# GpSimd's row writes in twos, an earlier one-hot and an earlier bias in a two-stage attention and expert kernel

## The reference, cut to what matters

```
def reference(x, ctx, g_xattn, g_ffn, Wq, Wk, Wv, Wo, Wg, bg, W1, b1, W2, b2):
    x = x + tanh(g_xattn) * xattn(layernorm(x), ctx, Wq, Wk, Wv, Wo)
    x = x + tanh(g_ffn)   * ffn(layernorm(x), Wg, bg, W1, b1, W2, b2)
    return x

# xattn: 16 heads of 16. For each token the scores are between the 16 dims of Q and the
# 16 dims of K (a 16 x 16 softmax for each token), then values, then @ Wo.T
# ffn: 8 experts, each token goes to one:
    logits = xf @ Wg + bg ; idx = argmax(softmax(logits))
    h = gelu(xf @ W1[idx] + b1[idx]) ; out = h @ W2[idx] + b2[idx]
```

## Time and profile before

| | us |
|---|---|
| median of 3 runs | 291.73 (291.23 to 291.84) |
| the profiled execution | 290.77 |
| its span, first to last instruction | 288.9 |
| PE busy | 275.6 (95%) |
| DVE busy | 211.3 (73%) |
| POOL busy | 130.4 (45%) |
| ACT busy | 102.9 (36%) |
| granted TensorE clock | 0.998 |

### The profile page before, as it was taken

How to read it: one execution, slowest core, us unless ns; L and a number is a source line. 1 busy time by engine, 2 the same in 40 slices (tenths; PEclk the granted TensorE clock), 3 DMA queues, 4 the chain that set the end, 5 groups by cost and what they waited for, 6 DMA issues and landing times.

```text
span 288.9 us, 9745 instructions
## 1 busy us (share of the span) xinstructions
PE 275.6 (95%) x3185; PEld 219.2 (76%) x3186; DVE 211.3 (73%) x613; ACT 102.9 (36%) x258; POOL 130.4 (45%) x156
## 2 busy tenths in 40 slices
PE   8999999999999999999999999799987999999990
PEld 7667777677776776777767777578976988998980
DVE  7667667787796786878778778788876875765661
ACT  2120311302203113031130321337664776776750
POOL 9623032243524525336254452702754554455565
PEclk9999999999999999999999999999999999999999
DMA  7955355476664755647656634414244344433311
GB/s 233 297 163 161 71 138 146 127 205 171 192 178 144 224 175 182 208 122 225 170 174 226 193 103 135 126 42 117 84 149 133 112 151 143 121 113 124 97 71 40
DMA packets 31242, 43.24 MB, mean 150 GB/s; under 512 B 7662, under 2 KB 18543, under 8 KB 31217
## 3 DMA queue, kind: packets, MB, share of 16 engines
q1 hardware_dynamic: 17760, 21.35, 26.7%
q10 hardware_dynamic: 10048, 12.99, 15.1%
q0 software_dynamic: 3408, 8.59, 8.4%
HBM read 24.83 MB, written 10.60 MB: 123 GB/s over the span
## 4 chain that ended last, share of the span: by engine, by line
PE 75%; issue 7%; POOL 5%; DVE 5%; DMA 5%; ACTq 1%; ACT 1%; POOLq 0%; DVEq 0%
PE ps_qo L439 18%; PE ps_pr L410 18%; PE ps_av L484 11%; PE ps_so L465 9%; POOL out_rows L1467 5%; PE ps_av L670 3%; PE ps_so L651 3%; PE ps_to L670 3%; PE ps_tr L474 3%; PE ps_tr L651 3%; PE ps_to L497 2%; PE ps_pr L641 2%; DMA sb_kb<-sb_y_k 2%; DMA out_rows<-sb_q_n,sb_tok_i 2%; DVE sb_kb L1279 1%
## 5 line engine op out<-in xcount | busy, mean ns | idle before, releaser
L410 PE MATMUL ps_pr<-sb_wkv,sb_ct 128*128 128x512 f32 x120 | 57.7, 605 | 0.0
L718 ACT ACTIVATE sb_pe_x<-sb_pe_x 128x512 f32<-128x512 f32 x16 | 10.1, 631 | 111.9 <-DVE sb_pe_x L894 100.6
L1397 POOL TENSOR_SCALAR sb_ve<-sb_mv 128x2 f32<-128x2 f32 x16 | 3.5, 220 | 78.0 <-DVE sb_mv L853 75.2
L1411 POOL DMA_INDIRECT routed_rows<-sb_xs,sb_pos_i x32 | 32.7, 1023 | 12.5 <-issue 7.4
L410 PEld LDWEIGHTS ps_pr<-sb_wkv,sb_ct 128*128 128x128 f32 x120 | 20.5, 190 | 17.7 <-issue 17.3
L484 PE MATMUL ps_av<-sb_vb,sb_at 128*32 128x128 f32 x1024 | 31.8, 274 | 1.5 <-issue 1.5
L465 PE MATMUL ps_so<-sb_kb,sb_y_q 128*32 128x128 f32 x1024 | 31.2, 273 | 0.5 <-DMA sb_kb<-sb_y_k 0.5
L484 PEld LDWEIGHTS ps_av<-sb_vb,sb_at 128*32 128x32 f32 x1024 | 27.2, 110 | 5.1 <-issue 4.9
L439 PE MATMUL ps_qo<-sb_wog,sb_ot 128*128 128x264 f32 x120 | 29.6, 388 | 0.0
L439 PEld LDWEIGHTS ps_qo<-sb_wog,sb_ot 128*128 128x128 f32 x120 | 22.5, 190 | 9.2 <-issue 6.4
L465 PEld LDWEIGHTS ps_so<-sb_kb,sb_y_q 128*32 128x32 f32 x1024 | 28.0, 110 | 1.9 <-issue 1.5
(11 more groups left out here) (159 smaller groups left out, 493.0 us busy)
## 6 DMA issues: line engine op xcount, KB each, us to landing
sb_x<-x_in ACTq DMA_DIRECT2D x16, 256.0 KB, 3.5
sb_kb<-sb_y_k SPq DMA_DIRECT2D x124, 32.0 KB
sb_vb<-sb_y_v SPq DMA_DIRECT2D x120, 32.0 KB
sb_ct<-ctx_in ACTq DMA_DIRECT2D x14, 256.0 KB, 3.1
sb_xt<-xt_in_ ACTq DMA_DIRECT2D x14, 256.0 KB, 4.6
sb_xb<-routed_rows SPq DMA_DIRECT2D x25, 134.0 KB
sb_w_all<-w_in_ SPq DMA_DIRECT2D x4, 514.0 KB
sb_w<-w_in SPq DMA_DIRECT2D x4, 512.0 KB
```

The lines of the kernel that those rows point to most:

```text
L410: last = pe.matmul(pr[:, s * 512:(s + 1) * 512], lhsT=ct[i][:, kc, s, :], rhs=wkv[:, :, kc, :], start=(kc == 0), stop=(kc == KC - 1))
L718: act.activation(pe_x[:], pe_x[:], ACT.Exp, scale=float(H) ** -0.5).then_inc(exp_done, 1)
L1411: pool.indirect_dma_start(rows, bass.IndirectOffsetOnAxis(ap=row_numbers(batch)[:, c:c + 1], axis=0), rows_of(j)[:, s, :], None).then_inc( ...
```

## The change

Five edits.

1. In `end()` the power of pair 12 stands between the two pairs of batch 5's row writes, and the power of pair 15 between the first and the second row write of batch 6.
2. Row writes of batches 6 and 7 with an odd number count up a semaphore of their own, `routed_odd`. POOL waits after every second of them until the even one of the two has landed, for batch 6 as well, and before batch 7's row writes it waits for the store of block 2.
3. `pick_7` of batch 7 stands ahead of the normalization of block 7.
4. `prepare` of block 38 comes one slot earlier, ahead of block 35's finish; `YL_ORDER` follows.
5. The stores of blocks 16 to 31 are written out.

```diff
-YL_ORDER = (0, 2, 1)
+YL_ORDER = (2, 0, 1)
...
-            sp.wait_ge(routed, 32 * pairs)
+            sp.wait_ge(routed, 32 * pairs - 64)
+            sp.wait_ge(routed_odd, 64)
...
-                if known and b == blocks - AHEAD:
+                if known and b == blocks - AHEAD - 1:
                     prepare(blocks - 1)
...
             behind(3, 3, 0)
+            pick_7(m)
             ahead(4, 4, 0)
-            pick_7(m)
             behind(4, 4, 0)
...
-                route_tile(2 * (batch % 2) + i // 2, i % 2, batch)
+                route_tile(2 * (batch % 2) + i // 2, i % 2, batch, routed_odd if i % 2 else routed)
+
+            def late_routed(batch, i):
+                return 64 * (last_batch - 1) + 32 * (batch - last_batch + 1) + 16 * (i // 2 + 1)
...
-                for j in range(2):
-                    route(2 * ((m - 1) % 2) + j, m - 1)
+                route(2 * ((m - 1) % 2), m - 1)
                 pow_x1(n - 2, (n - 2) % 4)
+                route(2 * ((m - 1) % 2) + 1, m - 1)
                 pow_x1(n - 1, (n - 1) % 4)
                 pow_x1(n, n % 4)
-                for i in range(2):
-                    route_nth(m, i)
+                route_nth(m, 0)
                 pow_x1(n + 1, (n + 1) % 4)
-                for i in range(2, 4):
-                    route_nth(m, i)
+                route_nth(m, 1)
+                pool.wait_ge(routed, late_routed(m, 1))
+                route_nth(m, 2)
+                route_nth(m, 3)
+                pool.wait_ge(routed, late_routed(m, 3))
...
                 if b == 3:
+                    pool.wait_ge(stored[2], 16)
                     for i in range(4):
                         route_nth(last_batch, i)
                         if i % 2 == 1:
-                            pool.wait_ge(routed, 32 * pairs - 16 * (3 - i))
+                            pool.wait_ge(routed, late_routed(last_batch, i))
...
-            block_slots(pool, store_in_twos, 0)
+            for b in range(EARLY, blocks):
+                store(b, b % RING, b // RING)
+                if b % 2 == 1 and b < blocks - 3:
+                    pool.wait_ge(stored[(b - 1) % OUT], 16 * ((b - 1) // OUT + 1))
```

More of the change, by code:

```diff
@@ L1406, in pow_x1, with route_tile @@
                 pool.tensor_tensor(rows_of(j)[:, :, RSTD], ve1[:], neg_half[:], ALU.pow).then_inc(res_pow, 1)
-            def route_tile(j, s, batch):
+            def route_tile(j, s, batch, done):
                 c = 2 * (j % 2) + s
                 pool.indirect_dma_start(rows, bass.IndirectOffsetOnAxis(ap=row_numbers(batch)[:, c:c + 1], axis=0),
-                                        rows_of(j)[:, s, :], None).then_inc(routed, 16)
+                                        rows_of(j)[:, s, :], None).then_inc(done, 16)
             def route(j, batch):
@@ L1417, in route @@
                 for s in range(2):
-                    route_tile(j, s, batch)
+                    route_tile(j, s, batch, routed)
             def route_nth(batch, i):
@@ L1477, in _ @@
                         if i % 2 == 1:
-                            pool.wait_ge(routed, 32 * pairs - 16 * (3 - i))
+                            pool.wait_ge(routed, late_routed(last_batch, i))
                 elif b % 2 == 1:
                     pool.wait_ge(stored[(b - 1) % OUT], 16 * ((b - 1) // OUT + 1))
-            def store_in_twos(b, q, turn):
-                store(b, q, turn)
-                if isinstance(b, int) and b >= blocks - 3:
-                    return
-                if q % 2 == 1 and isinstance(b, int):
-                    pool.wait_ge(stored[q - 1], 16 * (turn + 1))
-                elif q % 2 == 1:
-                    wait_apart(pool, stored[q - 1], 16 * (turn + 1), passed_pool)
-            block_slots(pool, store_in_twos, 0)
+            for b in range(EARLY, blocks):
+                store(b, b % RING, b // RING)
+                if b % 2 == 1 and b < blocks - 3:
+                    pool.wait_ge(stored[(b - 1) % OUT], 16 * ((b - 1) // OUT + 1))
 def kernel(x, ctx_1024, g_xattn, g_ffn, L0_xattn_Wq, L0_xattn_Wk, L0_xattn_Wv, L0_xattn_Wo, L0_ffn_Wg,
```

1 line of the change is left out of this document (added).

## The result

| | before | after |
|---|---|---|
| median of 6 runs each, one chip | 291.78 us (291.23 to 293.33) | 296.9 us (292.86 to 298.45) |
| ratio after/before, 95% interval | | 1.0128 [1.0091, 1.0164] |
| profiled execution | 290.77 us | 292.86 us, the fastest of the six |
| its span and granted clock | 288.9 us, 0.998 | 291.0 us, 0.993 |

The account below looks back on a forecast made before the run. PE was taken to bound the block phase. Its 0.7 us gain before the ranks, all other terms 0, took 290.77 to 290.1 us profiled, 291.0 us on the runs' scale; range 289.0 to 292.6.

Parts of the forecast that it names:

- The store loop written out: POOL's stores of blocks 16 to 31: POOL gains 5.3 us (0 to 8.7), but the end gains 0 to 0.30, taken as 0.
- Rival 3: At the end, DVE's unexplained 3.19 us behind PE may come from POOL's backlog; level POOL returns 1 to 3 us; chance 0.13.
- The power, the one-hot and what PE gets of it: Before the ranks: waits of 0.92 and 0.36 us go, one-hot another 0.32 us sooner; PE gains 0.7 us (0 to 1.0).
- Rival 1: ACT's copy at 210.91 keeps its time or PE loses the gain at 219.96; 291.6 to 291.8 us, chance 0.27.
- the 212.6 that I had named as a sign of being wrong: Sign against the forecast: the gelu of block 5 still starting near 212.6 us in the new profile.
- The power of pair 12: Between batch 5's row writes: puts 1.1 us ahead of two, covered by SP's 3.1 us wait; cost 0, otherwise 1.1 us.
- The landing waits: POOL, batches 6 and 7: landings of 2.4 to 3.2 us, last row write unchanged; PE net 0, POOL gains 1.3 us or more.
- rival 2: Four landings of 4.2 us each delay batch 7's row writes and block 16; +1.5 us, 292.3 to 293.2 us, chance 0.15.
- the 229 that I had named: Sign against the forecast: block 16 fetched after 229 us in the new profile.
- The preparation of block 38: Near the end, 0.5 us instruction moved off block 36's last step; value 0, ends -0.6 and +0.4 if it awaits block 30's store.

Follow-up runs that it names:

- f2_landing_only: The kernel before with edits 1 and 2 alone (row writes in twos with landing waits, moved powers); 293.44 us, ratio 0.9993.
- f3_prepare_only: The kernel before with the preparation of block 38 moved ahead of block 35's finish, alone, store loop kept; 292.12 us, ratio 1.0015.
- g1_again: The kernel before with the store loop written out and two memsets spacing each pair of blocks 16 to 31, second run; 291.73 us, 0.9969 (first run 0.9971).
- e4_free: The changed kernel, stores written out, without the landing waits from block 16 on; 285.07 us, ratio 0.9889.
- e3_fill: The changed kernel, stores written out, with memsets of unused tiles slowing POOL by 0.77 us for each two blocks; 292.45 us, ratio 1.0119.
- e1_loop: The changed kernel with the stores of blocks 16 to 31 in the loop again, its other four edits kept; 292.77 us, ratio 1.0119.
- e1_again: Repeat on another chip of the changed kernel with the store loop put back; 293.13 us, ratio 1.0122.
- g2_again: The kernel before, store loop kept but its landing waits taken away, second run, on another chip; 295.56 us, ratio 1.0127.
- e7_old_prepare: The changed kernel with the preparation of block 38 where it was before; 295.09 us, ratio 1.0088.
- f1_unroll_free: The kernel before with the store loop written out and no landing waits from block 16 on; 295.67 us, ratio 1.0126.
- e5_unroll_prepare: The kernel before with the store loop written out and the preparation of block 38 moved earlier (edits 4 and 5); 294.32 us, ratio 1.0048.
- e2_again: The kernel before with only the store loop written out (edit 5), second run, on another chip; 295.44 us, ratio 1.0141.
- e2_unroll_only: The kernel before with only the store loop written out (edit 5), first run; 283.43 us, ratio 0.9842.
- e2_third: The kernel before with only the store loop written out (edit 5), third run, on another chip; 283.5 us, ratio 0.9801.

## Why the prediction was wrong

**The store loop written out: the step that failed.** I put its worth at 0 to 0.30 us and took 0. The durations were right: two stores take 2.98 and 2.67 us (247.23 to 250.21 to 252.88), and POOL waits 2.63 us for DVE at 258.12. What failed is that its worth hangs on neither engine's pace alone, and it has both signs. On chips A and D no signal is late, POOL's stores end the run, 3.4 to 5.9 us behind DVE where they are looped or spaced (I had taken it that "POOL's lateness has been worked off"), and the edit alone takes off 1.6 and 2.0%, 4.6 and 5.8 us. On B, C and E, and in the first comparison, five and more stores in a row at 1.3 to 1.5 us in the mean come with signals of PE that are 2 to 5 us late, and the edit alone, on chip C, costs 1.4%, about 4 us. Over all traces, 8 have such a wait of over 2 us between 246 and 270 us, and they are just those with dense stores there on these chips; before, f2_landing_only, f3_prepare_only and g1_again, with spaced stores, have none of over 2 us there, and the eight traces of chips A and D have none at all. Rival 3 held the right suspicion ("the transfers bunched by it, makes the signals late") and drew the wrong sign: I expected a level POOL to thin the stores out at the end, and it did (3.16 us came back), but the same bunching then arose 30 us sooner, with half the clock behind it. The 3.19 us for which the trace named no reason were a term of the sum, and I had left them without a price.

**The power, the one-hot and what PE gets.** The waits of 0.92 and 0.36 us went, as forecast, but what PE got of it there is 0.38 us and not 0.7. Rival 1's condition came close to holding: ACT's copy starts at 211.29 instead of 210.91 and the gelu of block 5 at 212.28, near the 212.6 that I had named as a sign of being wrong. The rest of the 2.0 us by which PE's work from 205 to 225 us grew came at 219.96, for which the sum had nothing. It came with edits 1 and 2: f2_landing_only, which lacks edit 3, has all of it (19.25 us), so the 0.32 us of the one-hot bought nothing that a trace shows. Which of the two edits it was, the earlier power or the spaced row writes, was not run; before, ACT's copy at 219.54 starts 0.93 us behind the end of the transposes that it waits for (218.23 + 0.38), right behind four indirect DMAs at one per 1.28 us (213.72 to 217.57), which speaks for the spacing. So the forecast's gain was found, and for the most part not by its mechanism.

**The power of pair 12.** No run has it alone. The first fetch starts at 192.69 us instead of 191.90, and 0.55 of these 0.79 us are there before it, at batch 5's first row write (181.95 against 181.40), so it cost 0.24 us at most against my 0.

**The landing waits.** The forecast (last row write no later) was wrong and rival 2's chain right as far as DVE: 3.25 us ahead of store 0, the last row write 2.6 us late, block 16 fetched at 229.17 instead of 227.89, after the 229 that I had named. The first landing alone took 5.2 us (213.14 - 0.30 - 207.60), over rival 2's 4.2. The price was 0.36 us on PE in the changed kernel, since PE was ahead by its gain, 0.99 in f2_landing_only, and 1.86 and 2.60 on chip A (e4_free, e3_fill). Rival 2's sum has a slip: 230.4 + 2.92 + 0.41 makes 233.7 and not 233.9, so its price was 1.3 us and not 1.5. Alone edits 1 and 2 came to 0.9993 on chip C.

**The preparation of block 38.** Value 0 held on chip C (1.0015 alone). The upper end of 0.4 did not hold: behind a late store queue it is 5.83 us (e1_loop and e1_again, looped) and 3.57 (e3_fill, written out but slowed), on chips where POOL's stores end the run all the same; f3_prepare_only, looped, on chip C, waits 0.29 us. In the changed kernel it cost nothing that the trace shows.

**The clock.** I had no term for it. PE's stalls of 2.92 us in the changed kernel, 3.26 in g2_again, 3.37 in e7_old_prepare and 4.15 in e1_loop are followed by matmuls at the lower level, and so are one of 2.60 in e3_fill and one of 2.17 in f1_unroll_free (2.2 us behind one of 2.72); one of 3.63 us in e5_unroll_prepare isn't (clock 1.00), nor are those of 2.12 and 2.40 in e2_again. Estimated from the mean clocks, it adds 1.7 us in the changed kernel and 10 x 0.34 = 3.4 in g2_again, in e7_old_prepare and in f1_unroll_free alike. It isn't what makes dense stores slower: the traced execution of e2_again (295.15 us) is as slow as its median, with a granted clock of 1.000.

**What stays open.** Why the signals are late, and whether it is POOL's issuing or the transfers in flight that bring them; no run separates the two. The traces show when, not where they are held: at PE, at the semaphores, or in a matmul that in truth ended later than recorded. And what sets chips A and D apart: the kernel before takes 290.15 and 290.24 us on them, 291.8 to 292.5 on the others, and it spreads wider there (287.3 to 295.6 us, with granted clocks of 0.976 to 0.992, where e2_unroll_only and e2_third have 0.995 to 1.000). Without a trace of it on these chips, how the gain of 1.6 to 2.0% divides between the store queue and that clock isn't known, nor where edits 1 to 4 lose their 1.2%. How edits 1 to 4 fare together on a chip with late signals was not run; edits 1 and 2, and edit 4, came out as no change on chip C, and edit 3 was not run alone.

**What is better than both.** On a chip like A or D, edit 5 alone, 1.6 to 2.0% faster, or the loop without its landing waits, 2.2% on chip D. On the others both lose. Written out and spaced (g1) is the one version that was not slower on either kind of chip, 0.9971 and 0.9969, each interval just reaching 1.

## What to carry to other kernels

When one engine's issues of transfers are closed up, look for waits for other engines that lie inside the dense run, and price the run itself; a wait "for nothing that the trace names" next to one is a term of the sum and not noise. Measure such a change on more than one chip before it is kept or dropped: here the same kernel is 2% faster on one and 1.4% slower on another. Before a long wait is called the cause, see whether the chain that ended last goes through it: the 5.83 us of e1_loop doesn't lie on it. And before an instruction that may wait is moved forward in an in-order queue, take its wait at the queue's present lag, not at the lag after the other edits have worked.
